# Rows of x in two transfers of 128 partitions a chunk, in place of four of 32, in a graph attention kernel

## The chip, the cores and the metric

The kernel runs on one core of one Trainium2 chip. The metric is the device time of one execution in microseconds (us), lower is better; it was taken in 3 runs before the change. The profile is that of one further execution.

## The reference, cut to what matters

```python
def _L0_gnn_ref(h, adj, W, a):                # N = 8192, 128 features, float32; adj is 8192 x 8192 int32
    Wh = h @ W
    s1 = Wh @ a[:128, 0];  s2 = Wh @ a[128:, 0]
    e = leaky_relu(s1[:, None] + s2[None, :], negative_slope=0.2)
    masked = where(adj > 0, e, -9e15)
    return elu(softmax(masked, axis=1) @ Wh)

h = maximum(_layernorm(x, axis=-1), 0.0)
return x + _L0_gnn_ref(h, adj, W, a)
```

The adjacency matrix is 268 MB and is read once. x is 4.2 MB and is read once too: it stays in on-chip memory, where it is normalised at the start and added to each band of outputs at the end.

## The kernel before, in words

**Tiling.** The 8192 rows of x are eight chunks of 1024. A chunk `k` lies in the tile `xs` as eight tiles of 128 rows (`STEPS = 8`), one row of 128 floats in each partition of a tile. The rows are not laid out in order. Row `k*1024 + a*256 + w*128 + y*4 + b` stands in partition `32*a + y` and in tile `8*k + 4*w + b`, with `a` from 0 to 3, `w` from 0 to 1, `y` from 0 to 31 and `b` from 0 to 3. The four rows of one `b` run lie behind each other in memory, so that one run is 2 KB. A `group` is the 32 partitions of one `a`.

**Bands and units.** The output rows are eight bands of 1024. A band reads the adjacency matrix in 16 units of 512 by 1024 words, two units to a chunk of source rows. A unit is 2 MB and goes into one of four slots of the tile `raw` by four transfers of 512 KB, one for each group of 32 partitions: `load_unit` (L188) issues groups 0 and 1 on SP's queue and groups 2 and 3 on ScalarE's (the queues are q1 for SP and q10 for ScalarE in the DMA views). ScalarE turns a unit to bytes (`form_gates`, L445), VectorE transposes it (`turn_unit`, L723) and forms the weights of one step out of it (`weigh`, L747; `weigh_half` and `weigh_other_half` in the first chunk), and TensorE multiplies eight tiles of weights by one tile of `wh` in each step (`multiply`, L1039; in the first chunk `multiply_half`, L1062). A chunk is eight steps. A slot is loaded again only when the unit in it has been turned to bytes.

**x on its way in.** `load_x(eng, k, group)` (L183) brings the 32 partitions of one group of chunk `k`, both halves `w`: 128 KB, 64 runs of 2 KB. Four of them fill a chunk, and each adds 16 to the semaphore `x_in[k]`, for which `statistics` (L616) waits with 64. Chunks 0 to 2 (`EARLY = 2`) come first: groups 0 and 1 on SP's queue and groups 2 and 3 on ScalarE's, ahead of the first unit of the adjacency matrix. Chunks 3 to 7 come on SP's queue alone by `load_rows` (L211): chunk 3 behind SP's half of unit 0, chunk 4 behind that of unit 2, chunk 5 behind unit 4, chunk 6 behind unit 6, chunk 7 behind unit 8.

**Order around it.** Each engine carries out its own list in the order of the code. ScalarE issues six transfers of x and its half of unit 0 (L395 to L398), then takes the deviations of chunk 0, normalises four tiles of it, and only then issues its half of unit 1 (L439). `first_words` (L481) waits for unit 0; `load_ahead` (L488) issues ScalarE's half of unit 2 behind it, and the half of unit `u + 2` behind the gates of unit `u`. VectorE takes the statistics of chunks 0, 1 and 2 before `second_words` (L727), which waits for unit 0 too. TensorE ends the first chunk, and starts the second when its weights are there, for which units 2 and 3 have to be landed, turned to bytes and transposed.

Of the kernel before, what the change touches and what calls it, by code (L numbers as in the profile page):

```python
# [20 lines left out]
QUAD = 4  # L21
SQ = 32
RUN = 256
WORDS = RUN // QUAD
WB = WORDS // SQ
CHUNK = 4 * RUN
STEPS = CHUNK // P
# [11 lines left out]
def graph_attention(nc, x, adj, w, a, out):  # L39
# [20 lines left out]
    with ExitStack() as ctx:  # L60
        def sb(name, shape, dt=F32):
            return ctx.enter_context(nc.sbuf_tensor(name, shape, dt))

        def sem(name):
            return ctx.enter_context(nc.semaphore(name))
# [4 lines left out]
        xs = sb("xs", [P, NT, F])  # L70
# [61 lines left out]
        x_in = [sem(f"x_in{k}") for k in range(CHUNKS)]  # L132
# [40 lines left out]
        g_eyes = obuf[:, 0:UNIT].rearrange("p (t q) -> p t q", q=P)  # L173


        x_runs = x.rearrange("(k a w y b) f -> a k y w (b f)", a=4, w=WB, y=SQ, b=QUAD)
        out_runs = out.rearrange("(k a w y b) f -> a y k w (b f)", a=4, w=WB, y=SQ, b=QUAD)
        r_runs = r_rows.rearrange("(k t) p -> k (t p)", t=TILES)

        adj_runs = adj.rearrange("(k q w x b) j -> w x b k q j", q=4, w=WB, x=SQ, b=QUAD)  # L180
        adj_tiles = adj.rearrange("(k a w y b) j -> a w b y k j", a=4, w=WB, y=SQ, b=QUAD)

        def load_x(eng, k, group):  # L183
            part = slice(group * SQ, (group + 1) * SQ)
            eng.dma_start(xs[part, k * STEPS:(k + 1) * STEPS, :].rearrange("p (w b) f -> p w (b f)", b=QUAD),  # L185
                          x_runs[group, k]).then_inc(x_in[k], 16)

        def load_unit(eng, band, unit, groups):  # L188
            chunk, half = unit // 2, unit % 2
            slot = unit % RAW_SLOTS  # L190
            for group in groups:
                first = chunk * CHUNK + group * RUN
                rows = adj_runs[half][:, :, bass.ds(band, 1), :, first:first + RUN]
                eng.dma_start(raw[group * SQ:(group + 1) * SQ, slot, :, :].rearrange("p (b q) j -> p b q j", q=4),  # L194
                              rows.rearrange("x b k q j -> x b (k q) j")).then_inc(raw_in[slot], 16)

        def store_band(eng, band, groups, signal):
            for group in groups:
                part = slice(group * SQ, (group + 1) * SQ)
                rows = out_runs[group][:, bass.ds(band, 1), :, :].rearrange("y k w c -> y (k w) c")  # L200
                eng.dma_start(rows, obuf[part, :].rearrange("p (w c) -> p w c", w=WB)).then_inc(signal, 16)

        def safe(eng):
            eng.wait_ge(flag_ready, 1)
            return eng.value_load(flag[0:1, 0:1], min_val=0, max_val=1) == 1
# [3 lines left out]
        @block.sync  # L209
        def _(sp):  # L210
            def load_rows(k):  # L211
                for group in range(4):
                    load_x(sp, k, group)

            sp.dma_start(wext[:, 0:F], w).then_inc(w_in, 16)
            for group in (0, 1):
                load_x(sp, 0, group)
            for k in range(2):
                sp.dma_start(a21[:, 1 - k:2 - k], a[k * F:(k + 1) * F, :]).then_inc(a_in, 16)  # L219
            for k in range(1, EARLY + 1):  # L220
                for group in (0, 1):
                    load_x(sp, k, group)
            for u in range(RAW_SLOTS):
                load_unit(sp, 0, u, (0, 1))
                if u % 2 == 0:
                    load_rows(EARLY + 1 + u // 2)

            def safe_path():
                def band_of_loads(band, half, rows=True):
                    for u in range(UNITS):  # L230
                        sp.wait_ge(gate_ready, band * UNITS + (u - RAW_SLOTS + 1))
                        load_unit(sp, band, u, (0, 1))
                        if u == UNITS - 4 and rows:

                            sp.wait_ge(r_stored, 16)
                            sp.wait_ge(weights_ready, band * BAND_STEPS + 1)
                            sp.dma_start(rbc[:, 1 - half, :], r_runs[bass.ds(band + 1, 1), :].to_broadcast([P, BAND]))\
                                .then_inc(r_in, 16)
                        if u == UNITS - 1:
                            sp.wait_ge(out_ready, band)  # L240
                            store_band(sp, band - 1, range(4), out_done)

                for u in range(RAW_SLOTS, UNITS):
                    sp.wait_ge(gate_ready, u - RAW_SLOTS + 1)
                    load_unit(sp, 0, u, (0, 1))
                    if u % 2 == 0 and EARLY + 1 + u // 2 < CHUNKS:
                        load_rows(EARLY + 1 + u // 2)
                band_of_loads(1, 1)
                with sp.Fori(1, BANDS // 2 - 1) as pair:
                    for half in range(2):  # L250
                        band_of_loads(pair * 2 + half, half)
                band_of_loads(BANDS - 2, 0)
                band_of_loads(BANDS - 1, 1, rows=False)
                for h in range(2):
                    sp.wait_ge(last_ready, h + 1)
                    for group in (0, 1):
                        part = slice(group * SQ, (group + 1) * SQ)
                        sp.dma_start(out_runs[group][:, BANDS - 1, h, :], obuf[part, h * UNIT:(h + 1) * UNIT])\
                            .then_inc(out_done, 16)
                sp.wait_ge(out_done, (BANDS - 1) * 64 + 128)  # L260

            def general_path():
                for k in range(EARLY + 1 + RAW_SLOTS // 2, CHUNKS):
                    load_rows(k)
                for k in range(RAW_SLOTS):
                    sp.wait_ge(raw_in[k], 64)
                with sp.Fori(0, BANDS) as k:
                    for t in range(TILES):
                        sp.wait_ge(g_adj_free, k * TILES + (t + 1))
                        for group in range(4):  # L270
                            sp.dma_start(adj_rows[group * SQ:(group + 1) * SQ, :],
                                         adj_tiles[group, t // QUAD, t % QUAD][:, bass.ds(k, 1), :]
                                         .rearrange("y k j -> y (k j)")).then_inc(g_adj, 16)

            with sp.If(safe(sp)):
                safe_path()
                sp.nop()
            with sp.Else():
                general_path()
                sp.nop()  # L280
            sp.nop()
# [111 lines left out]
        @block.scalar  # L393
        def _(act):
            for k in range(EARLY + 1):  # L395
                for group in (2, 3):
                    load_x(act, k, group)
            load_unit(act, 0, 0, (2, 3))  # L398

            def normalise(n, odd):  # L400
# [207 lines left out]
        def _(dve):  # L608
# [5 lines left out]
                dve.wait_ge(dve_chain, links[0])  # L614

            def statistics(n, part):  # L616
                dve.wait_ge(x_in[n], 64)
                for u in range(part * GROUP, (part + 1) * GROUP):
                    t = n * STEPS + u
                    ins = nc.vector.bn_stats(stats[:, t, :], xs[:, t, :])  # L620
                ins.then_inc(stats_done, 1)
# [29 lines left out]
            for part in range(2):  # L651
                statistics(0, part)
# [9 lines left out]
            for part in range(2):  # L662
                statistics(1, part)
# [7 lines left out]
            for part in range(2):  # L671
                statistics(EARLY, part)
# [540 lines left out]
```

## Time and profile before

| | us |
|---|---|
| median of 3 runs | 983.22 (982.25 to 983.26) |
| the profiled execution, its own time | 983.03 |
| its span, first to last instruction | 981.4 |
| TensorE matmul busy | 952.7 |
| VectorE busy | 844.5 |
| ScalarE busy | 528.9 |
| GpSimd busy | 59.7 |

Busy times of different engines overlap. PE is TensorE, DVE VectorE, ACT ScalarE, POOL GpSimd and SP SyncE; SPq and ACTq are the sequencers of SP and ACT as they issue transfers. Matmuls are pipelined, so a busy PE need not be PE at its peak.

### The profile page before, as it was taken

Reading aid. Unit: us, or ns where it says so; the run is one execution under the profiler, and the core shown is the slowest. Engines: PE = TensorE matmul, PEld = TensorE weight load, DVE = VectorE, ACT = ScalarE, POOL = GpSimd, SP = SyncE. Lnnn points to the kernel's source line nnn. Section 1 sums busy time; section 2 is a strip of 40 time slices with the busy share of each in tenths; the row PEclk is TensorE's granted clock in tenths of the full one; section 3 lists DMA queues with packets and bytes.
Section 4 is the critical chain, followed back from the end, with each engine's and each line's share of the span. In section 5 each row is a group of like instructions: output and inputs, shape, how many; then the busy total and the mean of one; then the engine's idle time right before and its main releaser. Section 6 shows DMA issues by size and latency. Waiting matters only on the chain.

```text
span 981.4 us, 21311 instructions
## 1 busy us (share of the span) xinstructions
PE 952.7 (97%) x8432; PEld 949.6 (97%) x8432; DVE 844.5 (86%) x841; ACT 528.9 (54%) x358; POOL 59.7 (6%) x140
## 2 busy tenths in 40 slices
PE   3999999999999999999999999999999999999996
PEld 3899999999999999999999999999999999999996
DVE  5899889898888988898888988889888998889884
ACT  3677845665456455465356555564544654465420
POOL 3755200000000000000000000000000000000000
PEclk9899999999999999999999999999999999999998
DMA  9999999999999999999979999999999999999700
GB/s 241 303 317 318 334 288 281 325 297 351 321 302 269 301 334 314 289 258 341 326 194 346 309 353 295 300 269 295 340 315 270 278 339 321 284 294 287 221 0 24
DMA packets 276950, 280.77 MB, mean 286 GB/s; under 512 B 9696, under 2 KB 272032, under 8 KB 276896
## 3 DMA queue, kind: packets, MB, share of 16 engines
q1 hardware_dynamic: 140976, 144.79, 53.4%
q10 hardware_dynamic: 135920, 135.32, 49.3%
q8 instruction: 27, 0.44, 0.2%
q14 instruction: 27, 0.22, 0.1%
HBM read 275.84 MB, written 4.23 MB: 285 GB/s over the span
## 4 chain that ended last, share of the span: by engine, by line
PE 94%; DMA 3%; SPq 1%; DVE 1%; ACT 0%; issue 0%
PE ps L1043 92%; DMA raw<-in_adj 3%; PE ps L1015 1%; SPq L185 1%; PE ps L1005 0%; ACT gate L450 0%; PE ps L1052 0%; SPq L194 0%; DVE big L868 0%; DVE big L879 0%; DVE obuf L882 0%; DVE weights L749 0%; DVE big L725 0%; PE ps L1027 0%; SPq L219 0%
## 5 line engine op out<-in xcount | busy, mean ns | idle before, releaser
L1043 PE MATMUL ps<-wh,weights 128*128 (+1 forms) x8064 | 906.6, 275 | 3.3 <-DVE weights L749 3.3
L1043 PEld LDWEIGHTS ps<-wh,weights 128*128 128x128 f32 x8064 | 904.6, 192 | 4.0 <-issue 3.5
L749 DVE SCALAR_TENSOR_TENSOR weights<-big,beta 128x1024 f32<-128x1024 f32 x504 | 636.1, 1274 | 106.5 <-PE ps L1043 104.9
L450 ACT ACTIVATE gate<-raw 128x4096 uint8<-128x4096 int32 x127 | 460.2, 3624 | 369.6 <-DVE big L725 291.7
L725 DVE STREAM_TRANSPOSE big<-gate 128x1024 int32<-128x1024 int32 x128 | 158.5, 1238 | 4.1 <-ACT gate L450 4.1
L477 ACT ACTIVATE big<-ps,rden 128x128 f32<-128x128 f32 x56 | 23.1, 412 | 12.2 <-issue 12.2
L478 ACT ACTIVATE big<-ps,rden 128x128 f32<-128x128 f32 x56 | 23.4, 418 | 0.0
L566 ACT ACTIVATE big<-big 128x512 f32<-128x512 f32 x2 | 1.3, 630 | 33.7 <-DVE big L868 33.7
L1066 PE MATMUL ps<-wh,weights 128*128 128x129 f32 x128 | 17.4, 295 | 0.8 <-DVE weights L737 0.8
L1066 PEld LDWEIGHTS ps<-wh,weights 128*128 128x128 f32 x128 | 16.5, 209 | 1.4 <-issue 1.2
L1015 PE MATMUL ps<-wext,big 128*128 128x130 f32 x128 | 17.4, 292 | 0.4 <-issue 0.4
L1015 PEld LDWEIGHTS ps<-wext,big 128*128 128x128 f32 x128 | 16.7, 209 | 0.8 <-issue 0.8
L620 DVE BATCH_NORM_STATS2 stats<-xs 128x6 f32<-128x128 f32 x64 | 13.6, 278 | 1.7 <-DMA xs<-in_x 1.5
L682 DVE TENSOR_TENSOR wh<-ps,wh 128x512 f32<-128x512 f32 x16 | 10.8, 676 | 2.0 <-ACT beta L427 1.8
L415 ACT ACTIVATE big<-ps 128x512 f32<-128x512 f32 x16 | 9.5, 592 | 4.4 <-PE ps L1005 4.2
L426 ACT ACTIVATE wh<-ps,bias 128x4 f32<-128x4 f32 x16 | 4.2, 262 | 12.4 <-PE ps L1015 12.4
L407 ACT ACTIVATE obuf<-xs,shift,scale 128x128 f32<-128x128 f32 x24 | 9.6, 488 | 0.0
L786 DVE TENSOR_TENSOR big<-big 128x1024 f32<-128x1024 f32 x7 | 8.5, 1220 | 0.0
L791 DVE TENSOR_TENSOR obuf<-big,xs 128x1024 f32<-128x1024 f32 x7 | 8.5, 1219 | 0.0
L737 DVE SCALAR_TENSOR_TENSOR weights<-big,beta 128x512 f32<-128x512 f32 x8 | 7.1, 913 | 1.4 <-PE ps L1066 1.0
L407 ACT ACTIVATE big<-xs,shift,scale 128x128 f32<-128x128 f32 x20 | 8.0, 484 | 0.0
L1005 PE MATMUL ps<-identf,big 128*128 128x128 f32 x32 | 5.6, 311 | 1.8 <-ACT big L407 1.8
(96 smaller groups left out, 139.4 us busy)
## 6 DMA issues: line engine op xcount, KB each, us to landing
raw<-in_adj ACTq DMA_DIRECT2D x256, 512.0 KB, 11.3
raw<-in_adj SPq DMA_DIRECT2D x256, 512.0 KB, 11.5
out_x<-obuf SPq DMA_DIRECT2D x28, 128.0 KB, 10.6
xs<-in_x SPq DMA_DIRECT2D x26, 128.0 KB, 11.3
big<-r_rows SPq DMA_DIRECT2D x6, 512.0 KB, 14.2
xs<-in_x ACTq DMA_DIRECT2D x6, 128.0 KB, 4.4
out_x<-obuf SPq DMA_DIRECT2D x4, 64.0 KB, 1.7
out_x<-obuf ACTq DMA_DIRECT2D x4, 64.0 KB, 1.9
```

The costliest lines, as they stand in the source:

```text
L185: eng.dma_start(xs[part, k * STEPS:(k + 1) * STEPS, :].rearrange("p (w b) f -> p w (b f)", b=QUAD), x_runs[group, k]).then_inc(x_in[k], 16)
L407: ins = nc.scalar.activation(xn[n % 2][:, odd * GROUP + u, :], xs[:, t, :], ACT.Identity, bias=shift[:, t:t + 1], scale=scale[:, t:t + 1])
L450: nc.scalar.activation(gate[:, u % GATE_SLOTS, :, :], raw[:, u % RAW_SLOTS, :, :], ACT.Sign)\
L477: nc.scalar.activation(hbuf[:, rows], columns, ACT.Copy, scale=by)
L478: ins = nc.scalar.activation(ebuf[:, rows], columns, ACT.Exp, scale=by)
L620: ins = nc.vector.bn_stats(stats[:, t, :], xs[:, t, :])
L682: nc.vector.tensor_tensor(to[:, :, :, 0:F], source[:, :, :, 0:F], to[:, :, :, F:FD].to_broadcast([P, 2, 2, F]), ALU.mult)
L725: return nc.vector.transpose(turned[:, chunk, :, half * UNIT:(half + 1) * UNIT], words)
L749: nc.vector.scalar_tensor_tensor(weights[:, v % WT_SLOTS, :], rbc[:, half, :], beta[:, bass.ds(jt, 1)], turned_bytes[:, chunk, v // QUAD, ...
L1015: ins = nc.tensor.matmul(product_banks(g)[:, u // 2, u % 2 * FE:(u % 2 + 1) * FE], ht[:, g % 2, u * P:(u + 1) * P], wext[:, :], start=True ...
L1043: ins = nc.tensor.matmul(acc[half][:, t // BANK_TILES, t % BANK_TILES, 0:FD], weights[:, u % WT_SLOTS, t * P:(t + 1) * P], moving, start=s ...
L1066: ins = nc.tensor.matmul(acc[0][:, t // BANK_TILES, t % BANK_TILES, 0:FD], weights[:, v % WT_SLOTS, t * P:(t + 1) * P], wh[:, v, 0:FD], st ...
```

## The change

`load_x(eng, k, w)` now brings one half `w` of a chunk for all 128 partitions: four tiles, 256 KB, 128 runs of 2 KB. Two of them fill a chunk, and `statistics` waits for 32. In chunks 0 to 2 the half 0 goes on SP's queue and the half 1 on ScalarE's; chunks 3 to 7 bring both on SP's. The source view is `x_halves[k, w]`, which has the dimensions `a` (4), `y` (32) and `(b f)` (512 words); the destination has the dimensions 128 partitions and 512 words. The same rows come to the same places.

```diff
-        x_runs = x.rearrange("(k a w y b) f -> a k y w (b f)", a=4, w=WB, y=SQ, b=QUAD)
+        x_halves = x.rearrange("(k a w y b) f -> k w a y (b f)", a=4, w=WB, y=SQ, b=QUAD)
-        def load_x(eng, k, group):
-            part = slice(group * SQ, (group + 1) * SQ)
-            eng.dma_start(xs[part, k * STEPS:(k + 1) * STEPS, :].rearrange("p (w b) f -> p w (b f)", b=QUAD),
-                          x_runs[group, k]).then_inc(x_in[k], 16)
+        def load_x(eng, k, w):
+
+            first = k * STEPS + w * QUAD
+            eng.dma_start(xs[:, first:first + QUAD, :].rearrange("p b f -> p (b f)"), x_halves[k, w])\
+                .then_inc(x_in[k], 16)
...
             def load_rows(k):
-                for group in range(4):
-                    load_x(sp, k, group)
+                for w in range(WB):
+                    load_x(sp, k, w)
 
             sp.dma_start(wext[:, 0:F], w).then_inc(w_in, 16)
-            for group in (0, 1):
-                load_x(sp, 0, group)
+            load_x(sp, 0, 0)
...
             for k in range(1, EARLY + 1):
-                for group in (0, 1):
-                    load_x(sp, k, group)
+                load_x(sp, k, 0)
...
             for k in range(EARLY + 1):
-                for group in (2, 3):
-                    load_x(act, k, group)
+                load_x(act, k, 1)
...
             def statistics(n, part):
-                dve.wait_ge(x_in[n], 64)
+                dve.wait_ge(x_in[n], 32)
```

## Rows read from the trace of the kernel before

**Rows 1.** The page: busy time by engine, and the chain by engine.

```profile
PE 952.7 (97%) x8432; PEld 949.6 (97%) x8432; DVE 844.5 (86%) x841; ACT 528.9 (54%) x358; POOL 59.7 (6%) x140
...
PE 94%; DMA 3%; SPq 1%; DVE 1%; ACT 0%; issue 0%
```

**Rows 2.** The chain of waits in order of time: start us, us, what.

```profile
11.06 17.73 DMA raw<-in_adj
...
29.44 15.22 DMA raw<-in_adj
...
44.68 3.63 ACT gate L450
...
48.33 1.26 DVE big L725
...
51.04 3.64 PE ps L1043 x16
...
68.97 3.57 PE ps L1043 x32
...
88.14 1.79 PE ps L1043 x16
...
97.52 7.15 PE ps L1043 x64
```

**Rows 3.** Waits in the first 51.1 us: who, us in total, times, longest.

```profile
ACT gate L450 <- DMA raw<-in_adj: 6.0, 3, 2.5
...
DVE gate L730 <- DMA raw<-in_adj: 4.9, 1, 4.9
```

**Rows 4.** Timeline of the start: start us, us, engine, line, what.

```profile
0.86 2.81 ACTq L185 DMA_DIRECT2D xs<-in_x  x6
...
3.19 1.99 SPq L185 DMA_DIRECT2D xs<-in_x  x4
...
3.71 1.41 ACTq L194 DMA_DIRECT2D raw<-in_adj  x2
...
6.21 1.65 DVE L620 BATCH_NORM_STATS2 stats<-xs 128x6 f32<-128x128 f32 x8 [1.45 <-DMA xs<-in_x]
```

**Rows 5.** The same view narrowed to one SP issue.

```profile
11.74 6.80 SPq L194 DMA_DIRECT2D raw<-in_adj  x1
```

**Rows 6.** Windows: busy of each engine, PEclk, DMA share, GB/s.

```profile
0.00:3.00 3.00, 0.00 (x0) 0.00 (x0) 0.00 (x0) 0.00 (x0) 1.33 (x9) 1.00 0.26 84
...
0.00:45.00 45.00, 29.07 (x191) 27.54 (x192) 31.06 (x96) 20.64 (x34) 25.65 (x60) 0.89 1.03 266
...
51.00:102.00 51.00, 50.96 (x442) 50.99 (x443) 47.13 (x75) 39.37 (x52) 26.38 (x61) 0.97 1.10 322
```

**Rows 7.** The windows view again, a stretch without loads of x.

```profile
110.00:120.00 10.00, 10.00 (x92) 10.00 (x91) 8.17 (x9) 9.04 (x12) 0.00 (x0) 1.00 1.10 345
```

**Rows 8.** DMA of the whole span: packets, then issues (KB each, us to landing).

```profile
DMA packets 276950, 280.77 MB, mean 286 GB/s; under 512 B 9696, under 2 KB 272032, under 8 KB 276896
...
raw<-in_adj ACTq DMA_DIRECT2D x256, 512.0 KB, 11.3
raw<-in_adj SPq DMA_DIRECT2D x256, 512.0 KB, 11.5
...
xs<-in_x SPq DMA_DIRECT2D x26, 128.0 KB, 11.3
...
xs<-in_x ACTq DMA_DIRECT2D x6, 128.0 KB, 4.4
...
r_rows<-rt ACTq DMA_DIRECT2D x1, 32.0 KB, 10.5
```

**Rows 9.** DMA from 2.5 to 3 us.

```profile
DMA packets 155, 0.18 MB, mean 364 GB/s; under 512 B 28, under 2 KB 79, under 8 KB 155
```

**Rows 10.** DMA from 27 to 29 us.

```profile
DMA packets 408, 0.41 MB, mean 205 GB/s; under 512 B 8, under 2 KB 408, under 8 KB 408
...
q1 hardware_dynamic: 342, 0.34, 93.2%
```

## The prediction

> **What bounds the kernel now.** I read the page's busy times first: TensorE is busy for 97% of the span and makes up 94% of the chain that ended last, DMA 3% [rows 1]. Next the chain in order of time, to see where that 3% lies. From 51.04 us on it is TensorE without a gap. Before that it is the adjacency matrix on its way in: 17.73 us of DMA to 28.8, 15.22 us to 44.7, then the gates of unit 3 (3.63), its transpose (1.26), the first full weights, and TensorE at 51.04 [rows 2]. So a change to loads counts if it moves the landing of unit 3 at 44.7 us, or if it makes a later unit come after TensorE wants it. The waits of the start say the same: ScalarE's gates and VectorE's first words wait for `raw` [rows 3]. Last the DMA share: 1.03 of 16 engines over the first 45 us at 266 GB/s, 1.10 at 322 GB/s from 51 to 102 us [rows 6]. The 16 DMA engines have no slack to hide work in at the start, and little in the first band. After chunk 7 of x is in, x is not loaded again, and the last seven bands can't change.
>
> **The instructions.** Chunks 0 to 2 lose three issues of 0.45 us on each queue: ScalarE's six take 2.81 us and SP's four take 1.99 [rows 4], so both queues reach unit 0 about 1.4 us earlier (3.71 becomes about 2.3 on ScalarE). That is the gain that the issue side offers, and only until the DMA engines are saturated. VectorE's wait goes from 64 to 32 in units of the same transfers and costs nothing. Chunks 3 to 7 lose two issues each on SP, which is a queue ahead of its data (one issue of it sat 6.80 us for room [rows 5]); worth nothing.
>
> **The transfers.** Bytes, runs of 2 KB and places are unchanged. What does change is how a transfer can be shared out over DMA engines. Today every one is shared over all 16: the packets under 512 B are 9696, and the issues are 590 (544 in the four large groups shown, 46 in the seven others), and 590 x 16 = 9440 completion packets leave 256, which are the 256 single words of `a` [rows 8]. But each of those transfers begins, on both sides, with a count of 32, 64 or 128, in the source as in the destination. The new source begins with a count of 4 (`a`): the 128 rows of a half are four blocks of 32 with a jump between blocks, and no single stride covers them. No transfer of the trace begins with a count under 16, so the trace doesn't show what is done with it. The bounds are: shared over 16 as before, or cut only along the outermost count of both sides, which with 4 in the source and 128 in the destination gives four engines, one per block. I take four, because all the sharing seen so far could have been made along that first count alone, and 4 can't be cut into 16 without looking into the second count too.
>
> The trace bears out only the half of this that concerns counts of 32 and more. The Trainium skill, page "DMA: Bandwidth & Descriptors", section "Why a DMA increments its semaphore by 16 and not by 1", states the rule outright: the engine count is the largest number up to 16 that divides the slowest dimension of both patterns, and on these queues it is the lowest-numbered engines that are used. By it the sum would be the one that follows.
>
> **The cost with four engines.** In units of what one engine carries: a chunk of x is 0.524 MB, so 32.8 KB on each of 16 before, and 131.1 KB on each of the four after. A unit of the adjacency matrix is 2.097 MB, 131.1 KB on each of 16, before and after. Ahead of unit 3, or in the same queues, stand chunks 0 to 4 of x and units 0 to 3. The four engines must therefore move 9 x 131.1 = 1180 KB before unit 3 is complete, where each engine had 5 x 32.8 + 4 x 131.1 = 688 KB.
>
> Rate of one engine: the best half microsecond of loads of x shows 364 GB/s, 22.8 for one engine [rows 9]; the best ten microseconds of adjacency alone show 345, or 21.6 [rows 7]; the mean of the first 45 us is 266, or 16.6 [rows 6]. Data starts to flow at 2.2 us (26% of a 3 us window [rows 6]). So unit 3 lands at 2.2 + 1180/22.8 = 54.0, at 2.2 + 1180/21.6 = 56.8, or at 2.2 + 1180/16.6 = 73.3, against 44.7 now: 9.3, 12.1 or 28.6 us later. I take 21.6. The low mean of today comes with all 16 engines working into the same place: from 27 to 29 us SP's queue works nearly alone, into partitions 0 to 63 only, and the 16 busy engines together get just 205 GB/s [rows 10]. With four engines behind and twelve ahead, the total rate is 1180 x 4 plus 524 x 12 KB in 54.6 us, or 202 GB/s, well under what the core takes, so the four should run near their own best. The same arithmetic applied to the kernel before, 2.2 + 688/21.6 = 34 us instead of 44.7, shows how far it can be too kind, and is why the upper end stays in the range.
>
> The chain behind unit 3 (6.4 us to TensorE at 51.04) moves with it. In the meantime chunk 0 of the products isn't the limit: unit 0 lands about 2.2 + 4 x 131.1/21.6 = 26.5 us instead of 20.4, unit 1 about 8 to 10 us later than at 28.8, both less late than unit 3. ScalarE may be held at issue, since three transfers of x put 96 packets into each of four rings where there were 24, and the one full ring of today cost 6.80 us [rows 5]; the deviations of chunk 0 and the half of unit 1 are behind it on ScalarE, VectorE's statistics are behind x anyway (they start at 6.21 after a wait for x [rows 4]), and all of this must be done by unit 0 at 26.5. I count nothing for it; if that cover is gone it is 2 to 4 us.
>
> Then the first band. Chunks 1 to 4 of products each want the next two units, and x of chunks 5, 6 and 7 comes among units 4 to 9. One chunk's load is 3 x 131.1 = 393 KB on the four engines: 18.2 us at 21.6, or 19.6 at the 20.1 that 322 GB/s make [rows 6]. TensorE's own pace from chunk 1 to chunk 4 is 51.04 to 102.9 (97.52 plus three steps of 1.79), 51.8 us for three chunks [rows 2]. Three loads take 54.6 us: unit 9 is 2.8 us late (at 22.8: none; at 20.1: 6.9). From unit 10 on there is no x, a chunk's load is 12.1 us, and the late start is kept but doesn't grow.
>
> Sum: 12.1 + 2.8 = 14.9 us on the profiled execution's own 983.03, or 998. That execution is 0.2 us from the median, so no correction. Own range of this case: 9.3 with nothing late after gives 992; 28.6 + 6.9 gives 1018. I keep 990 to 1014 of it, since 28.6 supposes that the engines stay as slow when most of them are idle.
>
> **Rivals.**
> *All 16 engines still share each transfer, faster.* Its place is x of chunks 3 and 4, which SP issues group by group, and the starts of the queues. A transfer into 32 partitions reaches half the memory's width, 205 GB/s [rows 10], one into 128 the whole, 345 [rows 7]: 0.524 MB takes 1.5 us in place of 2.6, twice, so 2.1 us, and up to 1.4 more by earlier issues. It gives 980 to 983, near 981, and decides from the point at which the first count doesn't set the sharing. For it: each transfer seen today has all 16; against it: none of them begins with 4. The Trainium skill supports its size: "SBUF — State Buffer", section "Door 1: The DMA port swizzle", lets partitions 0 to 31 and 0 to 63 reach eight ports of 16; the 205 GB/s agree with it.
> *Nothing to be seen, 983.* 16 engines, and unit 3 goes on being set by when ScalarE issues its half (29.44, behind the gates of unit 1 [rows 2]) and not by bytes; or four engines whose extra load only fills time before that issue. Against the second: x of 0 to 3 stands ahead of unit 1, which itself releases that issue.
> *Four engines at the slow mean.* 1013 to 1018, the tail above.
>
> **Chances.** Four engines 0.76 (0.66 within 990 to 1014, the rest on both sides), 16 engines and faster 0.13, no difference 0.11. What a measurement of this kernel can tell from no change is 0.2%, about 2 us. Faster 0.13, same 0.11, slower 0.76. The range reaches down to 981 so that it takes in no difference and part of the faster case; the likeliest case's own is 990 to 1014.
>
> **What would show each step.** The packets under 512 B: 574 issues remain. With four engines they are 558 x 16 + 16 x 4 + 256 = 9248; with 16 they are 9440. Landing of x: above 8 us for the first on ScalarE's queue, where six had a median of 4.4 [rows 8], if four engines; under 5 otherwise. Unit 0's gates (L483) near 26 us, unit 3's (L450) near 57, TensorE's unbroken stretch from 63; GB/s in the first 45 us about 200 with a DMA share clearly under 1; two or three waits of TensorE for weights between 80 and 120 us, 3 us in all; from 170 us on the same 114.4 us a band. If x lands sooner than now and the share stays at 1, the forecast is wrong at its first step; if the 9248 are there and the time is within 4 us of before, it is wrong in what the start is bound by.

## The result, and the profile after

| | before | after |
|---|---|---|
| median, us | 983.24 (982.25 to 986.87, 4 runs) | 1074.8 (1072.24 to 1125.53, 4 runs) |
| ratio | | 1.091, 95% interval 1.088 to 1.094 |
| span of the profiled execution | 981.4 | 1073.7 |
| DVE busy | 844.5 | 841.5 |

The ratio leaves out runs more than 1.5% above the fastest of their kernel; some kernels below spread by more than that of themselves and have no ratio.

The forecast was 998 with a range to 1014. The direction was right, the size was not: 91 us in place of 15 (92.3 between the two profiled executions, which the parts below add up to). The main instructions are the same in number. TensorE is idle for 73.6 us more, and busy for 971.4 us in place of 952.7, since its granted clock falls between its waits. First the page of the changed kernel: busy, the span in 40 slices (26.8 us each), packets.

```profile
PE 971.4 (90%) x8432; PEld 964.2 (90%) x8432; DVE 841.5 (78%) x841; ACT 528.4 (49%) x358; POOL 52.6 (5%) x140
...
PEclk9777898999999999999999999999999999999998
DMA  7799999999999999999999999999999999999900
GB/s 145 159 175 180 176 188 221 218 251 254 271 258 354 346 321 274 348 302 291 269 324 302 285 294 306 353 300 277 284 342 302 291 268 346 304 293 271 295 0 22
DMA packets 276502, 280.77 MB, mean 261 GB/s; under 512 B 9248, under 2 KB 271584, under 8 KB 276448
```

Two things stand in it. The packets under 512 B are the 9248 forecast for four engines, where 9440 would be 16 ([rows 8] had 9696 for 590 issues). And the loads run at 145 to 188 GB/s for six slices, then at 218 to 271 for six more, up to some 320 us, though the last x was issued at 127.6 us and had landed by 154.4. Next the windows view (busy of PE, PEld, DVE, ACT, POOL, then PEclk, DMA share, GB/s), to be held against [rows 6].

```profile
0.00:45.00 45.00, 12.88 (x63) 11.54 (x64) 13.66 (x60) 10.89 (x23) 12.27 (x36) 0.92 0.70 147
65.00:160.00 95.00, 62.25 (x451) 60.73 (x451) 47.58 (x83) 36.02 (x50) 23.24 (x72) 0.80 0.96 182
160.00:220.00 60.00, 51.80 (x443) 51.45 (x442) 41.46 (x47) 34.05 (x47) 8.20 (x20) 0.94 1.10 217
220.00:300.00 80.00, 67.19 (x569) 65.20 (x568) 56.16 (x61) 37.00 (x31) 0.00 (x0) 0.98 1.10 259
310.00:370.00 60.00, 60.00 (x540) 60.00 (x539) 53.77 (x45) 32.58 (x9) 0.00 (x0) 1.00 1.10 338
```

From 160 to 220 us the DMA engines are as busy (1.10) as in the first band of before, and move 217 GB/s in place of 322. No load of x is left there. Two windows of the DMA view show what such a stretch is made of (kind, packets, MB, share of 16 engines).

From 182 to 184 us:

```profile
DMA packets 422, 0.43 MB, mean 215 GB/s; under 512 B 18, under 2 KB 421, under 8 KB 421
...
q1 hardware_dynamic: 365, 0.36, 94.7%
q10 hardware_dynamic: 56, 0.05, 14.7%
```

From 187 to 189 us:

```profile
DMA packets 424, 0.42 MB, mean 209 GB/s; under 512 B 16, under 2 KB 424, under 8 KB 424
...
q10 hardware_dynamic: 370, 0.36, 98.7%
q1 hardware_dynamic: 54, 0.05, 14.0%
```

The two queues take turns. SP's works nearly alone, then ScalarE's, and each nearly alone is the case of [rows 10]: 94.7% of 16 engines for 2 us over 365 packets is 83 ns each, where a share of 1.10 at 345 GB/s [rows 7] is 52 ns for 1024 B. It is not that one queue has nothing to do. Timeline of 176 to 200 us:

```profile
171.68 33.49 SPq L195 DMA_DIRECT2D raw<-in_adj  x7
...
180.52 1.29 ACTq L195 DMA_DIRECT2D raw<-in_adj  x2
```

SP sits at issue throughout, and ScalarE's two transfers of 180.52 are issued by 181.8, but its queue moves 56 packets from 182 to 184 us. A queue with transfers outstanding nearly stands still while the other works; no run shows why. It is the rule here and not the two windows alone: in 50 of the 60 stretches of 1 us from 160 to 220 us, one of the queues has under 30% of the 16 engines' time.

Last the places in time. Timeline rows of the start, and the chain from the second chunk to band 2:

```profile
0.87 2.78 ACTq L186 DMA_DIRECT2D xs<-in_x  x3
3.67 6.43 ACTq L195 DMA_DIRECT2D raw<-in_adj  x2
5.54 12.82 SPq L195 DMA_DIRECT2D raw<-in_adj  x2
14.99 1.65 DVE L618 BATCH_NORM_STATS2 stats<-xs 128x6 f32<-128x128 f32 x8 [11.24 <-DMA xs<-in_x]
36.93 1.91 ACT L481 ACTIVATE gate<-raw 128x2048 uint8<-128x2048 int32 x1 [3.54 <-DMA raw<-in_adj]
82.22 3.62 ACT L448 ACTIVATE gate<-raw 128x4096 uint8<-128x4096 int32 x1 [16.26 <-DMA raw<-in_adj]
88.58 3.78 PE L1041 MATMUL ps<-wh,weights 128*128 128x129 f32 x16 [5.21 <-DVE weights L747]
```

```profile
42.12 19.30 DMA raw<-in_adj
...
78.73 22.60 DMA xs<-in_x
...
103.47 5.86 PE ps L1041 x32
...
181.14 18.75 DMA raw<-in_adj
...
223.79 6.81 ACTq L195
...
372.83 0.49 PE ps L1050 x3
373.33 114.36 PE ps L1041 x1024
```

The chain of before has band 2 here:

```profile
281.05 114.36 PE ps L1043 x1024
```

Unit 3 is at its gates (L448) at 82.22 in place of 44.68 [rows 2], TensorE starts the second chunk at 88.58 in place of 51.04: 37.5 us. The last statistics of x begin at 154.4 us. Just before, TensorE takes the products of chunk 4 at 150.24, which it had taken at 89.77: by then 60.5 us are lost. Band 2 starts at 373.33, and at 281.05 before: 92.3. So 37.5 us go at the start, 23 more while x still comes, and 32 when there is no x any more. A band from there on is 114.85 us in both.

Two things in this chain are not the rate of the loads itself. TensorE's granted clock was 0.80 of full from 65 to 160 us, where TensorE was busy for only 62.25 of 95 us; on the chain 32 products took 5.86 us in place of 3.57 [rows 2], so at least 2.3 us of the 23 are the clock. And from 219 to 290 us the chain no longer goes through landings but through ScalarE at issue (the 6.81 us above is the longest piece): ScalarE is held at the issue of its next half, and its gates come late for that.

### The profile page after: what moved, and what is told of

Same layout as the page of the kernel before. It is cut to its first block, busy times and chain, and to the rows that moved or that the text cites. A ratio compares the mean times of both kernels' runs of the same rounds, so it can differ in the third digit from the quotient of the medians.

```text
span 1073.7 us, 21295 instructions
## 1 busy us (share of the span) xinstructions
PE 971.4 (90%) x8432; PEld 964.2 (90%) x8432; DVE 841.5 (78%) x841; ACT 528.4 (49%) x358; POOL 52.6 (5%) x140
## 2 busy tenths in 40 slices
DMA packets 276502, 280.77 MB, mean 261 GB/s; under 512 B 9248, under 2 KB 271584, under 8 KB 276448
## 4 chain that ended last, share of the span: by engine, by line
PE 71%; DMA 12%; SPq 6%; ACT 4%; ACTq 4%; DVE 1%; issue 1%
PE ps L1041 71%; DMA raw<-in_adj 9%; SPq L195 4%; ACTq L195 4%; ACT gate L448 4%; SPq L186 3%; DMA xs<-in_x 2%; DVE weights L747 0%; PE ps L1050 0%; ACTq L466 0%; ACT big L405 0%; ACT big L476 0%; ACT big L475 0%; DVE big L866 0%; DVE big L877 0%
## 5 line engine op out<-in xcount | busy, mean ns | idle before, releaser
L1041 PE MATMUL ps<-wh,weights 128*128 (+1 forms) x8064 | 919.6, 277 | 33.6 <-DVE weights L747 33.6
L1041 PEld LDWEIGHTS ps<-wh,weights 128*128 128x128 f32 x8064 | 915.3, 194 | 37.3 <-DVE weights L747 23.8
L448 ACT ACTIVATE gate<-raw 128x4096 uint8<-128x4096 int32 x127 | 460.4, 3625 | 457.4 <-DVE big L723 245.8
L1064 PEld LDWEIGHTS ps<-wh,weights 128*128 128x128 f32 x128 | 17.8, 221 | 17.9 <-DVE weights L741 11.8
L1003 PE MATMUL ps<-identf,obuf 128*128 128x128 f32 x32 | 6.5, 349 | 8.2 <-ACT big L413 7.0
L1003 PEld LDWEIGHTS ps<-identf,obuf 128*128 128x128 f32 x32 | 5.1, 184 | 8.6 <-issue 7.1
L1003 PEld LDWEIGHTS ps<-identf,big 128*128 128x128 f32 x32 | 4.6, 171 | 5.1 <-issue 3.2
## 6 DMA issues: line engine op xcount, KB each, us to landing
raw<-in_adj SPq DMA_DIRECT2D x256, 512.0 KB, 12.1
```

The lines of the kernel that those rows point to most:

```text
L448: nc.scalar.activation(gate[:, u % GATE_SLOTS, :, :], raw[:, u % RAW_SLOTS, :, :], ACT.Sign)\
L1003: ins = nc.tensor.transpose(ps[:, xt_bank(g), u * P:(u + 1) * P], xn[g // 2 % 2][:, g % 2 * GROUP + u, :], identf[:, :])
L1041: ins = nc.tensor.matmul(acc[half][:, t // BANK_TILES, t % BANK_TILES, 0:FD], weights[:, u % WT_SLOTS, t * P:(t + 1) * P], moving, start=s ...
L1064: ins = nc.tensor.matmul(acc[0][:, t // BANK_TILES, t % BANK_TILES, 0:FD], weights[:, v % WT_SLOTS, t * P:(t + 1) * P], wh[:, v, 0:FD], st ...
```

## The experiments

Times are medians in us; the kernel before had 982.3 to 984.3 beside them. Where there is no ratio, all runs are given. Several edits bring other rows into a partition, so the output differs; bytes and packets of data don't.

**One stride.** The changed kernel with a source of 128 runs in order.

```diff
-x_halves = x.rearrange("(k a w y b) f -> k w a y (b f)", a=4, w=WB, y=SQ, b=QUAD)
+x_halves = x.rearrange("(k w p b) f -> k w p (b f)", w=WB, p=P, b=QUAD)
```

> The changed kernel with one edit: the source of a half chunk is 128 runs of 2 KB with one stride (rows in order), so both sides begin with the count 128. Other rows of x land in each partition, so the output is that of rows in another order. Theory A (the first count of 4 confines each load of x to four DMA engines, and that is the whole loss): 9440 packets under 512 B, 980 to 984 us, x packets near 90 ns. Rival B (a transfer that writes 128 partitions, or 256 KB at a time on these queues, is what is slow, whatever the count): 9440 packets too, but still above 1040 us.

983.25 (10 runs), ratio 0.9997, interval 0.9985 to 1.0010, and 9440 small packets. The whole loss hangs on the four blocks of the source: 128 partitions at a time on 16 engines gain nothing and lose nothing.

**Eight blocks of 16.**

```diff
-... a=4, w=WB, y=SQ, ...
+... a=8, w=WB, y=SQ // 2, ...
```

> The changed kernel with the source cut as eight blocks of 16 runs instead of four of 32 (other rows of x land in a partition). Theory A, engines used are the first count: 574 issues, 558 x 16 + 16 x 8 + 256 = 9312 packets under 512 B, and 66 KB of a chunk of x on each of eight engines, half the extra load: 1000 to 1035 us. If the loss only came with fewer than some number of engines: 983. Rival B: the same 1075 as with four.

1044.75 (1037.99, 1051.52), ratio 1.0625 (1.054 to 1.071). The packets are those of eight engines:

```profile
DMA packets 276566, 280.77 MB, mean 267 GB/s; under 512 B 9312, under 2 KB 271648, under 8 KB 276512
```

The first count is the engine count: 4, 8 and 16 (from 128) each gave their own number. The time is above the expected 1000 to 1035. An engine's share of a chunk is 65.5 KB here, 32.8 more than with 16 engines, and with four it is 98.3 more: a third of the extra bytes, not half as the expectation had it, costs 61 of 91 us. The loss isn't in proportion to the extra bytes of an engine.

**Four engines, 32 partitions.** The kernel before with 64 KB transfers whose source is four blocks of 8 runs, and its control with one stride.

```diff
+x_blocks = x.rearrange("(k c a w y b) f -> a k w c y (b f)", c=4, a=4, w=WB, y=SQ // 4, b=QUAD)
...
+for w in range(WB):
+    first = k * STEPS + w * QUAD
+    eng.dma_start(xs[part, first:first + QUAD, :].rearrange("p b f -> p (b f)"), x_blocks[group, k, w])
```

> The kernel before, x in transfers of 32 partitions and 64 KB (eight a chunk), whose source begins with four blocks of 8 runs that no one stride covers (other rows of x land in a partition). It puts the same 131 KB of a chunk on each of four engines as the change does, but the four engines write 8 partitions each, next to each other. 64 issues of x: 558 x 16 + 64 x 4 + 256 = 9440 packets under 512 B, against 10208 with 16 engines. Theory A, the loss is the bytes on four engines alone: as slow as the change, 1050 to 1090. Theory C, in the change the four engines also stand in each other's way, since partitions 0 to 31 and 32 to 63 are written at the same time: x packets near 85 ns here against 160 to 170 in the change, and 995 to 1030 us.

> The control of the one before: the same eight transfers of 64 KB a chunk, the right rows, source with one stride, so 16 engines. 10208 packets under 512 B. It pays 32 more issues than the kernel before (six more on ScalarE ahead of unit 0, some 2.8 us). Both theories: 983 to 989 us.

1086 and 1121 against 986.78 for the control (ratio 1.0034, 1.0020 to 1.0048), small packets 9440 and 10208. As slow as the change, or slower, and the 2 KB packets of x took as long: 168 ns on average from 65 to 160 us, in the change 170. So theory C falls: that the blocks 0 to 31 and 32 to 63 are written at once is not what costs. The 32 more issues are worth 3 us.

**Early half and late half.** Only chunks 0 to 2, then only chunks 3 to 7, in the new form.

```diff
+                load_half(sp, k, 0)
...
+                load_half(act, k, 1)
... (the other kernel)
+                for w in range(WB):
+                    load_half(sp, k, w)
```

> Only chunks 0 to 2 of x come in two transfers of 128 partitions (4-block source, six transfers on four engines); chunks 3 to 7 come as before. Theory A (each chunk that four engines carry costs its own time, the first ones wait at the start, the later ones in the first band): three of eight chunks, 15 to 40 us: 998 to 1023. Theory D (once the two queues have been thrown out of step by full rings they stay so, and the loads run at some 215 GB/s long after the last load of x on four engines): 1015 or more, with 210 to 220 GB/s still after 60 us, when no such transfer is left.

> The other half: chunks 0 to 2 as before, chunks 3 to 7 in two transfers on four engines, on SP's queue alone. Theory A: 1035 to 1060, the rest of the 91 us, so that this and the early half add up to the change. Theory D: nearly the whole loss by itself, 1055 to 1075, and the two halves add up to clearly more than 91 us, since the slow stretch that follows is paid once however it was begun.

Early: 1041.12 and 1104.37. Late: 1062.93 and 1067.88, ratio 1.083 (1.077 to 1.089). The smaller of the early runs is 57 us over before and the late half 81, together 138 at the least against 91 for both. Costs that each chunk pays for itself would add up; these don't. The late half alone buys nearly the whole loss. The profiled run of the early half (1104.37) shows more: it was back at 311 GB/s from 260 to 400 us, and fell again.

```profile
800.00:900.00 100.00, 91.71 (x774) 89.78 (x773) 73.42 (x64) 44.03 (x27) 0.00 (x0) 0.97 1.12 244
```

There the kernel before has 298 GB/s and TensorE busy for the whole 100 us. No load on four engines is near, so the low rate can come back long after them; what brings it back is open. The run of 1086 above has 245 GB/s from 900 to 1050 us too.

**Wide transfers of the adjacency matrix.** What comes slowly without any x is `raw`. Each of its 512 KB transfers now writes 128 partitions, four 1 KB packets each, in place of 32 with 16 each; first with x as before, then with the changed x.

```diff
-adj_runs = adj.rearrange("(k q w x b) j -> w x b k q j", q=4, w=WB, x=SQ, b=QUAD)
+adj_runs = adj.rearrange("(k w q p) j -> w p k q j", q=4, w=WB, p=P)
...
-eng.dma_start(raw[group * SQ:(group + 1) * SQ, slot, :, :]...
+eng.dma_start(raw[:, slot, group * 4:(group + 1) * 4, :], rows.rearrange("p k q j -> p (k q) j"))
```

> The kernel before with other data for the adjacency matrix: each of the four 512 KB transfers of a unit writes all 128 partitions (source begins with 128 rows of one stride), 1 KB packets, as many bytes and packets as before. The rows land in wrong places, so the output is not that of the reference. Theory D needs that the 89 to 92 ns packets of a queue alone come from 16 engines writing into 32 partitions; then here no stretch falls to 205 GB/s, packets stay near 50 ns, and the time is 975 to 983. If slow packets have another source (memory, the rate of one queue): stretches of 205 GB/s as before and 983.

> The changed kernel with the same wide transfers of the adjacency matrix as in the run before (wrong rows, as there). x still on four engines, 9248 packets under 512 B. Theory A, the four engines' own bytes are the loss, or full rings are: little changes, above 1050. Theory D: what remains is my predicted cost alone, the bytes on four engines at their full rate, 990 to 1015; adjacency packets near 50 ns, and x packets near 85 to 100.

985.89 (ratio 1.0014, 0.9999 to 1.0029) and 1010.7 (1.0272, 1.0242 to 1.0301). With wide transfers the same four-engine loads of x cost 25 us, not 91, and no low rate stays behind them. The second kernel's windows:

```profile
0.00:45.00 45.00, 18.09 (x85) 16.26 (x86) 17.93 (x71) 10.88 (x23) 17.42 (x41) 1.00 0.67 184
45.00:120.00 75.00, 62.14 (x489) 60.81 (x488) 54.67 (x95) 43.91 (x57) 28.30 (x81) 0.91 0.92 259
120.00:190.00 70.00, 69.44 (x623) 69.28 (x622) 59.80 (x75) 48.80 (x54) 9.50 (x20) 1.00 1.02 326
```

Its last x is in by 120 us, and from there it moves 326 GB/s at a share of 1.02, where the changed kernel moved 217 at 1.10. Unit 3 reaches its gates at 63.4, and at 43.0 with 16 engines: 20.4 us for the four engines at the start.

**One disturbance in band 1.** The kernel before, and some 160 us in, behind SP's half of unit 4 of band 1, four extra transfers into spare memory; the control has the one-stride source.

```diff
+if isinstance(band, int) and band == 1 and u == 4:
+    for k in range(4):
+        sp.dma_start(junk[:, k, :], x.rearrange("(k a w y b) f -> k w a y (b f)", ...)[k, 0]).then_inc(junk_in, 16)
... (the control)
+        sp.dma_start(junk[:, k, :], x.rearrange("(k w p b) f -> k w p (b f)", ...)[k, 0]).then_inc(junk_in, 16)
```

> The kernel before, all of x as it was, and in band 1 (some 180 us in, TensorE long without a gap) four extra transfers of 256 KB into spare memory on SP's queue behind unit 4, each with the 4-block source, so 128 packets of 2 KB in each of four rings. Theory A, the cost is that of the packets alone: 131 x 2 KB at 21.6 KB/us, 12 us on four engines, mostly behind the slots already loaded: 983 to 995, and the loads back at their pace within 20 us. Theory D, the queues fall out of step and stay so: a stretch of 205 to 260 GB/s of 50 us and more behind the last extra packet, with TensorE waiting again and again: 1000 to 1060.

> Its control: the same four extra transfers, source of 128 runs with one stride, so on all 16 engines, 32 packets each. Both theories: 983 to 988, since TensorE is the bound there and 1 MB takes 3 us of 16 engines. If it is slow too, not four engines but any extra load on one queue at this place does it.

1098.85 (1081.84, 1098.75, 1098.94, 1100.75) against 983.36 for the control (ratio 1.0007, 0.9991 to 1.0022). 1 MB of extra loads on four engines costs 98 to 117 us in four runs, more than either theory allowed; on 16 it costs nothing. Windows of the disturbed kernel:

```profile
100.00:150.00 50.00, 50.00 (x451) 50.00 (x450) 42.88 (x49) 33.65 (x48) 6.54 (x14) 1.00 1.11 310
200.00:300.00 100.00, 81.23 (x630) 79.75 (x631) 64.56 (x55) 40.32 (x26) 0.00 (x0) 0.87 1.10 226
300.00:400.00 100.00, 82.20 (x670) 80.05 (x669) 64.12 (x56) 40.41 (x26) 0.00 (x0) 0.95 1.13 215
400.00:500.00 100.00, 82.86 (x671) 81.45 (x670) 61.09 (x53) 39.79 (x11) 0.00 (x0) 0.91 1.12 227
500.00:600.00 100.00, 89.87 (x776) 88.37 (x775) 76.80 (x65) 47.53 (x28) 0.00 (x0) 0.98 1.11 266
600.00:700.00 100.00, 90.11 (x780) 89.72 (x779) 78.72 (x68) 53.21 (x30) 0.00 (x0) 0.93 1.08 295
700.00:800.00 100.00, 100.00 (x897) 99.85 (x896) 88.44 (x74) 56.32 (x31) 0.00 (x0) 1.00 1.10 304
```

Four loads of 256 KB at 160 us still show at 600. In between ScalarE's gates come every 9.8 us (353.08, 362.86), where TensorE wants a unit each 7.15, and the queues take turns within that period. From 353 to 355 us, then from 358 to 360:

```profile
q10 hardware_dynamic: 372, 0.37, 98.3%
q1 hardware_dynamic: 56, 0.06, 14.3%
```

```profile
q1 hardware_dynamic: 373, 0.37, 98.7%
q10 hardware_dynamic: 59, 0.05, 14.4%
```

**How large a push, and with wide transfers.** One and two extra transfers in place of four; and the full four in the kernel with wide adjacency transfers.

> One extra transfer of 256 KB with the 4-block source in place of four, 32 packets in each of four rings; adjacency as in the kernel before. Theory D says that a push out of step is enough, however begun: if one transfer suffices, 1040 to 1100; if the push has to fill the rings (an SP issue sat 6.8 us for room at the start before), 983 to 990. Theory A: 984.

> Two extra transfers with the 4-block source in band 1, between one (984 us, nothing) and four (1082 to 1101). If the rings must be full for long enough to hold SP up: 64 packets on each of four rings are below or at the limit: 984 to 1000. If it is a matter of chance whether the queues fall out of step: anything from 984 to 1100, with a spread between its runs.

> The disturbance of band 1 (four extra transfers of 256 KB with the 4-block source) in the kernel whose adjacency transfers write all 128 partitions (wrong rows, as in the two runs before with that edit). Theory D, the long loss needs that each queue writes one half of the partitions only: the loads are back at 46 to 51 ns a packet right behind the extra packets, and the time is 984 to 996. If what stays is anything else in the queues (rings, the order of the two sequencers): above 1060, as with 32-partition transfers.

One: 984.08 (ratio 1.0012, 0.9996 to 1.0027). Two: 1039.79 (1038.54, 1041.05; 1.058, 1.053 to 1.063). Four: 1099. Four with wide transfers: 983.69 (1.0004, 0.9986 to 1.0023), with this row for the stretch that was at 226 GB/s:

```profile
200.00:300.00 100.00, 100.00 (x896) 99.85 (x895) 87.95 (x74) 52.47 (x16) 0.00 (x0) 1.00 1.02 328
```

Two transfers do harm, and their two runs lie within 2.5 us of each other, so the expectation of 984 to 1000 is refuted, and the spread that chance would bring is not seen. The expectation rested on SP being held long enough. But SP was not held at those two issues (1.30 us for both, 13.96 for the four), and the loads still lost their rate; so a held issue there is not what begins it.

The disturbance costs 98 to 117 us with transfers of 32 partitions and nothing with transfers of 128.

**Mixed halves.** Can the queues be made robust by giving each both halves of the partitions? SP's brings groups 0 and 2, ScalarE's 3 and 1, with the disturbance and without.

```diff
-load_unit(sp, band, u, (0, 1))
+load_unit(sp, band, u, (0, 2))
...
-load_unit(act, ..., (2, 3))
+load_unit(act, ..., (3, 1))
```

> The full disturbance (four transfers), but SP's queue brings groups 0 and 2 of each unit and ScalarE's 3 and 1, so each queue writes into both halves of the partitions, one transfer after the other. Theory D in its narrow form (one transfer of 32 partitions at a time is what is slow, whichever queue it is on): still above 1060. In its wide form (one queue for one half is the fault): 984 to 1010, and the layout would be the robust one.

> The kernel before with groups 0 and 2 on SP's queue and 3 and 1 on ScalarE's, and no disturbance. If the 1198 us with the disturbance came from it: 983 to 990 here. If a pair of queues that both write into both halves runs badly by itself (whenever they stand at groups of the same half): above 1050, and the present layout, one half for each queue in step, is what makes 345 GB/s possible.

1197.82 (1.217, 1.207 to 1.228) and, undisturbed, 1126.49 (1115.35, 1137.63). Worse by itself, and not by taking turns: from 300 to 400 us both queues are at work all the time (56.4% and 54.2%, and neither under 30% in any of the 100 stretches of 1 us, where the disturbed kernel above has 76 such), at 272 GB/s where TensorE wants 293. So with transfers of 32 partitions one queue for each half is not the fault. Both at work and each on its own half is what the rows of 345 GB/s have.

**A version meant to beat both.** As before, but ScalarE's queue brings groups 2 and 3 of chunks 3 to 7 as well.

```diff
-for group in range(4): load_x(sp, k, group)
+for group in (0, 1): load_x(sp, k, group)      # ScalarE: groups (2, 3), behind its half of the same unit
```

> A version meant to beat both: as before in four transfers of 32 partitions, but of chunks 3 to 7 SP's queue brings groups 0 and 1 and ScalarE's queue groups 2 and 3, right behind their halves of the same unit, so that the two queues carry the same packets and stay side by side. If the stretches of 205 GB/s at the start (27 to 29 us) come from SP's queue being the longer one, unit 3 lands up to 3 us sooner: 979 to 982. If the start is set by when ScalarE issues its halves: 983. Two more issues ahead of ScalarE's deviations could cost 1 us: 984.

983.94 (10 runs), ratio 1.0001, 0.9988 to 1.0014. Nothing. No version here beats the kernel before.

## Why the prediction was right on the engines and wrong in the cost

**The engine count: right.** 9248 small packets, to the packet, and 9312 with eight blocks. The Trainium skill, page "DMA: Bandwidth & Descriptors", section "Why a DMA increments its semaphore by 16 and not by 1", gave that rule; the counts of 4, 8 and 128 agree.

**The issue side: right that it is worth nothing.** The one-stride kernel has all of it, with 16 engines, and is at 983.25. So the rival near 981 was too hopeful by 2 us even with 16 engines: there unit 3 is at its gates at 44.03, against 44.68 before, and the time is the same. Its 345 GB/s for a transfer into 128 partitions was read from [rows 7], which are two queues with transfers of 32 partitions each.

**The rate of the four engines at the start: mis-sized, 12.1 us forecast and 37.5 measured.** The step that failed is "so the four should run near their own best". The 1180 KB of an engine were in at 82.2 us, not at 56.8: 14.8 KB/us from 2.2 us on, where 21.6 was taken, and less even than the 16.6 of the slow rival. A 2 KB packet of x would take 95 ns at 21.6 and a 1 KB packet of `raw` 47. By the packet records of the traces up to the gates of unit 3 they took 140 and 85 ns on average, and 119 and 64 in the kernel before. An estimate from these: 320 packets of x and 512 of `raw` are 88 us of one engine in the change, and 80 and 512 are 42 us before; measured were 80.0 and 42.5 from the 2.2 us on (the packets of two queues can overlap on an engine: a share goes up to 1.10). So the bytes were right, and the price of a packet was not. That is also why the same arithmetic gave 34 us for before in place of 44.7, which the prediction noted and didn't follow up. The other twelve engines don't help: they have to wait at times (share 0.70 over 45 us), as the two sequencers sit at issue (SP 12.82 us over two issues, ScalarE 6.43, rows above), for which the prediction counted nothing. With wide adjacency transfers the packets took 108 and 59 ns, and the same term is 20.4 us. So by difference some 17 of the 37.5 come with the narrow transfers of `raw`.

**The first band while x comes: 2.8 us forecast, 23 measured.** The same failure: a packet of x took 170 ns and one of `raw` 86 from 65 to 160 us, at 182 GB/s, in place of 322 in the first band of before. At least 2.3 of the 23 are TensorE's clock.

**After the last x: nothing forecast, 32 us measured.** "The late start is kept but doesn't grow" is the sentence that the trace refutes, and the largest lesson. The prediction had the row for it, 205 GB/s with SP's queue alone [rows 10], and used it only as a sign of what would get better. It is the price of one queue alone. Once the queues take turns, the loads run at 210 to 217 GB/s, less than the 293 that TensorE's 7.15 us a unit ask for, so nothing is left over to catch up with. That four loads in band 1 bring it about and wide transfers take it away is shown. How a few loads on four engines bring two queues, both with transfers outstanding, to take turns is not. The Trainium skill, page "SBUF — State Buffer", section "Door 1: The DMA port swizzle", has 32 or 64 partitions of one half reach 8 of the 16 ports. This case's 205 to 215 GB/s for one queue nearly alone, against 345 for both, fit that. But the wide transfers also read other rows of the matrix than the narrow ones, so that it is the writing and not the reading side of the narrow shape is argued, not shown. Open too is what ends the state, and what brought it back in the early half: it faded between 220 and 300 us in the changed kernel and between 500 and 700 in the disturbed one.

**The chances.** 0.76 went to slower, which it was, but even the slow tail of that case ended at 1018. It came from the slowest mean of before; no row of before shows the queues taking turns for long, so no row bounded it.

## What to carry to other kernels

Look at the first count of a transfer's source: with 128 partitions on the other side it set how many DMA engines carried it here (4, 8, 16), and the packets under 512 B count them. Where two queues each fill one half of the partitions by transfers of 32, their full rate hangs on both moving at once. Here two extra transfers on four engines were enough to end that, and it cost for hundreds of microseconds after they were gone. Price a load by how long its packets take in a trace of this kernel, not by the best rate seen. When loads have little slack, don't price a disturbance by its bytes: ask what rate the loads have once the queues have lost step, and whether that rate is enough to catch up.

## What the hardware showed that I had not expected

- Two states of the same loads, same bytes and packets: 345 GB/s and about 215, both with the DMA engines busy all the time (share 1.10 and 1.13).
- A step: 32 packets of 2 KB more on each of four engines did nothing, 64 cost 57 us, 128 cost 98 to 117.
- A queue with issued transfers can nearly stand still (14.7% of the 16 engines' time) while the other takes 94.7%.
- With wide transfers the loads kept up at a DMA share of 1.02 in place of 1.10, and TensorE's time did not move, since it is the bound.
